# Attention inside one fused layer: the products with the values, two steps at a time

## The reference

```
Q, K, V = x W^T, split into 16 heads of 8          (rotary embedding on Q and K)
scores  = Q K^T / sqrt(8), causal
attn    = softmax(scores) V, then W_O
x       = layernorm(x + attn)
gates   = softmax(x Wg + bg), the best 2 of 8 experts, renormalised
x       = layernorm(x + sum over the two of gate * (gelu(x W1 + b1) W2 + b2))
```

## Time and profile before

| | |
|---|---|
| Runs | 766.18, 769.34, 774.05 us; median 769.34 |
| Profiled execution | a span of 795.5 us; no other time of its own is given |
| Mean granted clock of PE in it | 0.925 |
| Busy | PE 670.2 us (84%), DVE 570.4 (72%), ACT 443.8 (56%), POOL 351.2 (44%) |
| DMA | 83.75 MB, mean 105 GB/s |

### The profile page before, as it was taken

One profiled execution on the slowest core, in us unless ns is written; L12 is line 12 of the kernel. 1 busy time (PEld: TensorE's weight loads), 2 busy tenths in 40 slices (PEclk: granted clock), 3 DMA queues, 4 the chain that ended last, 5 costly groups with the idle time before them and its releaser, 6 DMA issues.

```text
span 795.5 us, 19063 instructions
## 1 busy us (share of the span) xinstructions
PE 670.2 (84%) x5560; PEld 362.2 (46%) x5561; DVE 570.4 (72%) x1386; ACT 443.8 (56%) x843; POOL 351.2 (44%) x664
## 2 busy tenths in 40 slices
PE   7879999999898897989898998898698766999950
PEld 3344333334343332434333334332198756888840
DVE  8977888888879886787988898986255621222295
ACT  2343676666555665555567656567456433655535
POOL 5862224223353484153447516248423555444460
PEclk9985999999989999898999999999799977999995
DMA  8883455011010120101012001000276745687935
GB/s 288 271 287 130 141 136 157 18 49 49 2 49 2 56 79 22 49 1 49 6 55 83 28 33 48 1 8 29 66 217 185 198 123 151 186 212 204 298 89 158
DMA packets 67358, 83.75 MB, mean 105 GB/s; under 512 B 9266, under 2 KB 46776, under 8 KB 67264
## 3 DMA queue, kind: packets, MB, share of 16 engines
q1 hardware_dynamic: 62912, 74.04, 31.5%
q0 software_dynamic: 4352, 8.53, 3.1%
HBM read 55.77 MB, written 26.90 MB: 104 GB/s over the span
## 4 chain that ended last, share of the span: by engine, by line
PE 53%; DVE 21%; issue 10%; ACT 4%; SPq 3%; DMA 3%; POOL 2%; another core or an unknown queue 1%; DVEq 0%; ACTq 0%; POOLq 0%
PE banks L779 15%; DVE mx L1226 12%; PE banks L729 9%; PE banks L759 6%; PE banks L837 5%; PE banks L848 5%; PE banks L724 3%; ACT region L895 2%; PE banks L671 2%; PE banks L788 2%; DMA region<-pairs 1%; DVE region L1363 1%; PE banks L686 1%; ACT region L931 1%
## 5 line engine op out<-in xcount | busy, mean ns | idle before, releaser
L1226 DVE TENSOR_REDUCE mx<-banks 128x1 f32<-128x512 f32 (+3 forms) x640 | 365.2, 631 | 52.3 <-PE banks L729 47.6
L895 ACT ACTIVATE region<-banks 128x1024 f32<-128x1024 f32 (+3 forms) x256 | 201.5, 841 | 136.8 <-PE banks L759 132.1
L729 PE MATMUL banks<-region 64*128 64x512 bf16 (+3 forms) x768 | 188.4, 340 | 13.8 <-DVE mx L1226 10.8
L759 PE MATMUL banks<-region 64*128 64x512 bf16 (+3 forms) x768 | 139.2, 339 | 12.0 <-ACT region L895 5.5
L779 PE MATMUL banks<-region 128*32 128x512 f32 (+3 forms) x1024 | 118.8, 537 | 0.9 <-POOL region L1518 0.8
L1528 POOL DMA_INDIRECT results<-region,dest x72 | 71.5, 993 | 105.8 <-DVE region L1363 83.8
L895 ACT ACTIVATE cs_sb<-banks 128x1024 f32<-128x1024 f32 (+2 forms) x128 | 91.2, 759 | 43.2 <-PE banks L759 42.4
L724 PE MATMUL banks<-mask_sb,half_sb 64*128 64x128 bf16 (+1 forms) x384 | 83.3, 249 | 25.4 <-DVE mx L1226 19.8
L1518 POOL TENSOR_SCALAR_AFFINE_SELECT region<-region 128x256 f32<-128x256 f32 x160 | 63.8, 407 | 84.0 <-ACT region L895 80.6
L848 PE MATMUL banks<-region,w1e 128*128 128x128 f32 x576 | 84.0, 293 | 20.0 <-ACT region L923 15.2
L1357 DVE TENSOR_TENSOR region<-banks,w1e 128x128 f32<-128x128 f32 x72 | 20.9, 290 | 105.6 <-PE banks L837 60.0
(11 more groups left out here) (204 smaller groups left out, 705.9 us busy)
## 6 DMA issues: line engine op xcount, KB each, us to landing
w1e<-in_w SPq DMA_DIRECT2D x72, 322.0 KB
region<-stack_q SPq DMA_DIRECT2D x64, 112.0 KB
region<-stack_k SPq DMA_DIRECT2D x32, 224.0 KB
region<-pairs SPq DMA_DIRECT2D x72, 66.0 KB
region<-results SPq DMA_DIRECT2D x8, 512.0 KB, 4.8
stack_q<-x_sb SPq DMA_DIRECT2D x8, 384.0 KB, 3.7
stack_k<-x_sb SPq DMA_DIRECT2D x8, 384.0 KB, 4.6
stack_q<-x_sb SPq DMA_DIRECT2D x8, 256.0 KB, 3.6
```

Of the source, the lines that this page charges most:

```text
L729: last = mm(ring[:, bank, m * n:(m + 1) * n], qst[rows, v % NG, sb_ // 4, slot_, sb_ % 4 * P:(sb_ % 4 + 1) * P], kst[rows, v % NG, slot_, ...
L759: last = mm(score[:, slot_, par, 0:n], kst[rows, u % NG, slot_, j * P:(j + 1) * P], qst[rows, u % NG, c, slot_, s0 - c * CH:s0 - c * CH + ...
L895: nc.scalar.activation(probs[i % 6][:, :, 0:n], score[:, i % 2, :, 0:n], ACT.Exp, scale=SCALE).then_inc(exp_done, 1)
L1226: read(v.tensor_reduce(dst, src, AX.X, ALU.max, negate=True))
```

## The change

`PV` is no longer issued once in every step. An even step issues two at its end, of the two steps before, one right behind the other; an odd step issues none. The second of the two stands where it stood before, the first a step later. As a step's probabilities are then kept longer, there are eight buffers for them, the two new ones in 8 KB a partition of their own (`more_probs`), and ACT's exponential of a step waits for the `PV` of four steps before it, not three.

```diff
--- before.py
+++ after.py
@@ -169,8 +169,8 @@
             ev += items[half:]
             if u + 1 < NU and k in (first, NB - 1):
                 ev.append(("SPLIT", u + 1, int(k == NB - 1)))
-            if step:
-                ev.append(("PV", step - 1))
+            if step and step % 2 == 0:
+                ev += [("PV", step - 2), ("PV", step - 1)]
                 if (step - 1) % NB in C_LAST:
                     ev.append(("EV", 2 * ((step - 1) // NB) + C_LAST.index((step - 1) % NB)))
             for back in (0, 1):
@@ -190,7 +190,7 @@
             if u == NU - 1 and k == 4:
                 ev.append(("TA",))
     last = NU * NB - 1
-    ev += [("PV", last), ("EV", 2 * NU - 1), ("OT", 2 * NU - 1)]
+    ev += [("PV", last - 1), ("PV", last), ("EV", 2 * NU - 1), ("OT", 2 * NU - 1)]
     ev.append(("END",))
     for i, (_, events) in enumerate(sorted(after(B - 1).items())):
         ev += [("TILE", i)] + events
@@ -351,9 +351,11 @@
 
         qst = region[:, 0:4096].bitcast(BF16).rearrange("p (g c s n) -> p g c s n", g=NG, c=2, s=2)
         kst = region[:, 4096:8192].bitcast(BF16).rearrange("p (g s n) -> p g s n", g=NG, s=2)
+        more_probs = sb("more_probs", [P, 4 * CH])
         probs = [a[:, i, :, :] for a, n in ((region[:, 8192:12288], 4),
-                                            (cs_sb[:, :, :].rearrange("p a n -> p (a n)"), 2))
+                                            (cs_sb[:, :, :].rearrange("p a n -> p (a n)"), 2), (more_probs[:, :], 2))
                  for a in (a.rearrange("p (k w n) -> p k w n", k=n, w=2),) for i in range(n)]
+        PB = len(probs)
         vx = region[:, 12288:16384].rearrange("p (g t h c) -> p g t h c", g=NG, t=BT, h=GH)
         ot = sb("ot", [P, 2, CH])
         rden = sb("rden", [P, 2, 4 * GH])
@@ -777,7 +779,7 @@
                         for par in (0, 1):
                             h = 2 * slot_ + par
                             last = mm(pv[32 * h:32 * h + 32, s0 - c * CH:s0 - c * CH + n],
-                                      vx[:, u % NG, j, h, :], probs[(2 * e[1] + slot_) % 6][:, par, 0:n],
+                                      vx[:, u % NG, j, h, :], probs[(2 * e[1] + slot_) % PB][:, par, 0:n],
                                       start=(j == 0), stop=(k == C_LAST[c]),
                                       tile_position=(0, 32 * h), skip_group_check=True)
                     last.then_inc(pv_done, 1)
@@ -889,10 +891,10 @@
                     i = e[1]
                     n = B_STEPS[i // 2 % NB][3]
                     act.wait_ge(qk_done, at(i + 1, 2 * NB * NG))
-                    if i // 2 >= 3:
-
-                        act.wait_ge(pv_done, at(i // 2 - 2, NB * NG))
-                    nc.scalar.activation(probs[i % 6][:, :, 0:n], score[:, i % 2, :, 0:n], ACT.Exp,
+                    if i // 2 >= PB // 2:
+
+                        act.wait_ge(pv_done, at(i // 2 - PB // 2 + 1, NB * NG))
+                    nc.scalar.activation(probs[i % PB][:, :, 0:n], score[:, i % 2, :, 0:n], ACT.Exp,
                                          scale=SCALE).then_inc(exp_done, 1)
                 elif e[0] == "VALUES":
                     keep_values(e[1])
@@ -1514,7 +1516,7 @@
                     i = e[1]
                     pool.wait_ge(exp_done, at(i + 1, 2 * NB * NG))
                     pool.sem_inc(mask_turns, 1)
-                    block_ = probs[i % 6][:, :, 0:P]
+                    block_ = probs[i % PB][:, :, 0:P]
                     pp.affine_select(out=block_, in_=block_, compare_op=ALU.is_ge, fill=0.0, base=0,
                                      pattern=[[0, 2], [1, P]], channel_multiplier=-1).then_inc(masked, 1)
```

## The result

The changed kernel takes 824.26 us (median of 4 runs, 820.01 to 831.52) against 771.69 us of the kernel before on the same chip (766.18 to 777.0). The ratio is 1.070, with a 95% interval of 1.065 to 1.075: 53 us slower, where 19 were forecast, and outside the range. The profiled execution has a span of 823.9 us, near that median. That of before had 795.5 us, 24 above its own; nearly all of the surplus lies behind the attention, where the experts took 225 us from the last PV to the end, against 202 in this one and 200 to 204 in the later profiles. The stretch with PV is comparable: 496 us before, 543 us now.

The account below looks back on a forecast made before the run. The prediction took DVE to set the pace, with holes outgrowing PE's savings: +16 us for holes in 15 units, -1 for the last unit, +4 for the clock, so 769.3 + 19 = 788 us, range 762 to 810 us.

Parts of the forecast that it names:

- Where other work covers it: Units where DVE also has chains on a finished batch: these hide part of the longer block, leaving 0.5 us a unit.
- The term for the clock: Steps without PV leave PE waiting on DVE: 10 us more at half clock, costing 4 us.
- The longer block against a ring of three: Pairs delay row maximum products past DVE's three banks: larger holes, 1.6 us more a unit, between 0.8 and 2.8.
- the upper bound: Each pair's hole is its second block's present hole plus the first's pitch: 6.0 us a unit, 2.8 us more.
- The last unit: The unit without row maximum products, where PE and ACT alternate: keeps six saved block type changes, a gain of 1 us.
- the clock falls often: Rival: in steps without PV, PE waits on DVE, some 60 us more at half clock, 808 us; chance 0.15.
- Saved changes of block type: On PE, each pair drops one way into and one out of PV: 0.19 us, 18 us of PE time for 96.
- The rival that PE bounds: PE, not DVE, sets the time, so the 18 us saved show: 751 us; chance 0.15.
- the rule of draining: Changing PE's tiling mode drains the engine; by that alone, with PE as bound, the change gains the whole 18 us.
- The buffers: Two more probability buffers for ACT's exponentials: no exponential waits longer than before, costed at nothing.

Follow-up runs that it names:

- two PV apart: Changed kernel, but the two PV of an even step stand apart, one mid-step and one at its end: 787.91 us, ratio 1.021.
- short exponentials and pairs: Changed kernel with ACT's exponentials over only 64 columns of each part: 827.3 us, against 769.89 us for the order before with the same exponentials.
- DVE and ACT were out of the way: Row maxima and exponentials both cut to 64 columns: 700.95 us in the order before, 704.73 us in the order of the change.

## Why the prediction was wrong

**Direction and mechanism were right; the step that failed is "Where other work covers it", and with it the choice inside the bounds.** The term for the clock, 4 us, was too small as well. By the prediction's own steps:

- *The longer block against a ring of three.* Right, with bounds of 0.8 and 2.8 us a unit. Measured are 2.6 us in the undisturbed units (27.7 to 30.3), and after the pairs that begin with 512 columns, hole for hole, what the upper bound lists: 1.14, 1.29, 1.24 and 1.03 against 1.15, 1.34, 1.28 and 1.07. The value taken was 1.6, on the ground that a step without PV lets PE fill the ring and that the small pairs would give their holes back. They did not: holes of 0.61, 0.27 and 0.24 us stand there as before, with PE waiting for ACT ahead of the first of them. 7.5 units at 1.6 us made 12; the six units of that kind grew by 12.4. That this term came out right is luck: 1.6 us are far under the 2.6 of an undisturbed unit, and 7.5 units are more than the six.
- *Cover by chains.* 0.5 us a unit were forecast for 7.5 units, 4 us. The nine units with chains grew by 30.4 us, 3.4 each. This is the mis-sized term. With the 4 us that were forecast for the clock it stands at 8 against 30, so 22 of the 34 us that were missing. By DVE's idle time about half of the growth lies at the full clock, 15 us or 1.7 a unit, where 0.5 was forecast; the other half lies in time at half clock. Their chains do not stand behind a pair as a rule. The schedule puts a piece of them behind steps of both kinds, and some pieces take a bank of the ring that PE fills (line 819). One such unit, number 9, has 10.2 us at half clock in both kernels and grew by 1.4 us, from 37.8 to 39.2: there the cover was partly real. I had drawn the cover from the total length of such a unit, not from what DVE does just after a PV block, which rows of that unit would have shown.
- *The last unit.* Forecast -1 us, measured +5. "PE and ACT alternate there" was written down, but neither that a block of 1.86 us is as long as ACT's two exponentials (0.95 us each), after which ACT has nothing, nor that the clock could fall there. Single blocks in that unit give the 5 us back; most of them may be the clock's.
- *The clock.* The price of 0.40 to 0.47 us for each us at half clock held within a unit: in one kernel, units of the same work differ by 1.5 us for 3.4 us (two PV apart), or 1.6 us for 3.4 us (short exponentials and pairs, 30.9 and 29.3 us), 0.44 and 0.47. From run to run of the kernel before it is lower: over 50 runs the time rises by 0.24 us for each us at half clock, worked out from span and mean clock. The amount did not hold: 10 us more were forecast, 30 were measured in the 15 units of the profile. At 0.45 that is 14 us inside the 43, all of it in units with chains. By the mean clocks of the runs it is 46 us more in the whole kernel (90 and 137), so 11 to 21 of the 53 us, where 4 were forecast. No run takes the clock's part away alone, so these are estimates from those prices. So the rival "the clock falls often" came true in part, beside the holes and not in their place. The falls need no long block, as the kernel with PV apart shows; and steps without PV do not always bring them, as units 1, 2, 3 and 11 of the changed kernel stay at the full clock.
- *Saved changes of block type.* 0.19 us a pair forecast, 0.15 seen once DVE and ACT were out of the way, and no gain from it with them in place. The rival that PE bounds falls with that, and so does the rule of draining as a reason for a gain: the page "TensorEngine Tiling" of the Trainium skill (Key Properties) is borne out by the 0.9 us a unit, but the 18 us do not show in the time.
- *The buffers.* Nothing, as costed.

What stays open is which comes first in the units with chains, the longer holes or the falls of the clock, and why the reorderings with no longer block (PV apart, and PV ahead of the last pass A item) have more half clock than the kernel before.

## What to carry to other kernels

Where two engines hand each other work through a ring, ask of every block on the one how long the ring lasts the other, and take the whole excess as the cost, once for each block, unless a row shows what the waiting engine does in just that moment. An average share of other work says little: here the units with such work grew by more than those without it. Give the clock of PE a term of its own: here it is worth some 11 to 21 of the 53 us. When an engine is made faster by grouping, look at every consumer that runs dry meanwhile: here ACT stood behind DVE, and only with both out of the way did the saving appear, in the units without other work.

## What the runs showed of the hardware

- Two blocks of four 128 x 32 float32 products of 512 columns, one right behind the other, take 1.86 us; one block between matmuls of 64 x 128 takes 1.00 us, and 0.31 us pass from the start of the matmul before to its own.
- In the kernel with two PV apart the clock fell once in each of three units in a row, 30.7 us apart, for 3.4 us each time, so the three have the same length to 0.1 us. Falls of the clock can settle into step with a loop and then look like a fixed cost of it.
- The profiled execution of the kernel before was 24 us slower than its median, and behind the attention it took 225 us where the others took 200 to 204. When a span lies far from the median, compare stretches of the two profiles and not their spans.
